# Two waits for GpSimd's first residual sums, and four VectorE normalisations moved behind the last lr-weighted writes

## The chip, the cores and the metric

The kernel runs on one core of a Trainium2 chip. The metric is device time in microseconds, the median of several executions. Beside it there is one profiled execution with its own time.

## The reference

`x` has 4 sequences of 1024 rows with 128 features, all in float32. Cut to what matters here:

```python
h  = layernorm(x)                                  # no gain, no offset
# delta block on h
z  = layernorm(h) * dn_g + dn_b
q, k, v = split(z @ gates_w + gates_b, 3);  lr = z @ lr_w + lr_b
k  = k / norm(k)
A  = tril(k @ k.T, -1) + eye;   u = solve_triangular(A, v, lower=True)
y  = (q @ k.T) @ (lr * u)                          # all 1024 rows of a sequence
h2 = h + y @ out_w + out_b
h3 = h2 + relu((layernorm(h2) * mn_g + mn_b) @ w1 + b1) @ w2 + b2
x1 = x + h3
# expert block on x1, 8 experts
n  = layernorm(x1);  e = argmax(n @ gate_w.T)
out = x1 + (n + n @ expert_w[e])   # as the reference writes it: x1 + ffn(n)
```

## The kernel before, in words

The 1024 rows are cut into T = 8 tiles of 128 rows; a tile holds NS = 4 sequences side by side (`n` = 0 to 3; LOW is 0 and 1, HIGH is 2 and 3). TG is 4, half of T. Each engine has a program of its own, written out by hand in order; semaphores are the only links between them, and an instruction that waits holds everything behind it on its engine.

There are three stages. First, keys, Gram matrices and the triangular inverses are made. Then comes a recurrence over the tiles: per tile and sequence, TensorE reads the state with the keys (`ks`), VectorE makes the residual values `rv` (L885), TensorE multiplies with the tile's inverse (`w_`, L1288, counted by `w_mm`), the product and its copy scaled with the learning rate `lr` go to the tile `ww`, and TensorE adds key times `ww` onto the state and onto the sum `m` (`s_`, L1298). For the last tile, t = T - 1, only the part scaled with `lr` is needed: ScalarE writes it for LOW (L626), VectorE for HIGH (L939, counted by `lrw_last`). The sums go through ScalarE's copy L631 (`mm`), a product with `wqT`, a copy to `mw` (L634 on ScalarE for LOW, L942 on VectorE for HIGH), a product with `wo`, and an addition (L947), to `gn`, which holds all that the last stage needs of the recurrence.

The last stage goes tile by tile. `delta(t)` on TensorE multiplies with `gn`; VectorE adds the residual `h_all` (`h2_`, L954), takes statistics (`hstats` L960, `haggr` L966), ScalarE takes the root (`hroot`, L638), VectorE makes the scale (`hscale`, L971) and the bias `nb2` (`hbias`, L975, counted by `hnb_done`, one per sequence), ScalarE normalises (`tn_`, L649, in `k_all`), TensorE turns the result (`tT_`), ScalarE copies it (L655), and two matrices follow (`hid_`, L1369, and `out_`, L1104). VectorE adds them to `x_all` (`x1_`, L981). The eight experts' products (L1390) and VectorE's predicated copies (L1022), which pick one of them, fill most of the rest. Tile 0 is worked in halves, LOW and HIGH; the others whole.

GpSimd (POOL) prepares `x_all` for `x1_`: `xb2_(t)` (L347) adds the constant `b2s`, `xb_(t)` (L353) adds `h_all` once `h2_` of that tile or half is written (`h2_ready`), and `x1_` waits for it through `xb_ready`. Before the last stage the residual `h_all` = `(x - mean) * scale` has to be made again: GpSimd does it for LOW (L340), VectorE for HIGH (`h_(t)`, L890, two instructions of 128x128 per tile, counted by `h_dve`). `xb2_(t)` and `h2_(t)` wait for both. VectorE's `h_` calls stand in its loop over the recurrence's tiles TG to T - 1, two of them, that is four instructions, per tile.

In the loop below, `rv_all(t)` is four times L885 and `yb`, `zb`, `t12` are parts of the inverses of the next tile.

Of the kernel before, what the change touches and what calls it, by code (L numbers as in the profile page):

```python
# [17 lines left out]
def delta_block_kernel(  # L18
# [19 lines left out]
    NS, L, C = x.shape  # L38
    E, F, _ = expert_w.shape
    T = L // P  # L40
# [3 lines left out]
    TG = T // NG  # L44
# [18 lines left out]
    with ExitStack() as ctx:  # L63
# [3 lines left out]
        def sem(name):  # L67
            return ctx.enter_context(nc.semaphore(name))
# [3 lines left out]
        def tiles(bank):  # L72
            return ps[:, bank, :].rearrange("p (n c) -> p n c", n=NS)

        def rows(t):
# [111 lines left out]
        hst_done, hmv_done, hsd_done, hrr_done, hnb_done = (sem("hst_done"), sem("hmv_done"), sem("hsd_done"),  # L187
                                                            sem("hrr_done"), sem("hnb_done"))
# [44 lines left out]
        def span(of):  # L233
            return slice(of[0], of[-1] + 1)

        def upto(t, of):
            return NS * t + of[-1] + 1
# [61 lines left out]
        @block.gpsimd  # L299
        def _(pool):  # L300
            nc.gpsimd.memset(ident[:], 0.0).then_inc(zeroed, 1)
            nc.gpsimd.memset(cent[:], 1.0 / C).then_inc(zeroed, 1)
            nc.gpsimd.memset(onec[:], 1.0)
            nc.gpsimd.memset(epsc[:], EPS).then_inc(consts_ready, 1)
            pool.wait_ge(zeroed, 1)
            nc.gpsimd.affine_select(out=ident[:], in_=ident[:], compare_op=ALU.not_equal, fill=1.0, base=0,
                                    pattern=[[-1, P]], channel_multiplier=1).then_inc(ident_ready, 1)
            pool.wait_ge(ident_ready, 1)
            pool.wait_ge(zeroed, 2)

            nc.gpsimd.tensor_tensor(cent[:], ident[:], cent[:], ALU.subtract).then_inc(cent_ready, 1)
            for g in range(NG):
                nc.gpsimd.memset(xi[g][:], 0.0).then_inc(xi_ready, 1)
            nc.gpsimd.memset(da_all[0:Q, :, :, Q:2 * Q].rearrange("p t n c -> p (t n) c"), 0.0).then_inc(da_clear, 1)
            for t in range(5, T):
                last = nc.gpsimd.memset(tt_all[:, t], 0.0)
            last.then_inc(tt_clear, 1)

            for t in range(1, T):
                pool.wait_ge(rr_done, PART[t] + 1)  # L320
                for n in XH_POOL[t]:
                    nc.gpsimd.tensor_scalar(xh[:, t, n], x_all[:, t, n], mv[:, 0, t, n, 0:1], rr[:, t, 1, n:n + 1],  # L322
                                            ALU.subtract, ALU.mult).then_inc(xh_pool, 1)


            pool.wait_ge(g_loaded, 16 * 2)
            pool.wait_ge(v_loaded, 16 * 5)
            nc.gpsimd.tensor_scalar(bmean[:], dnb.broadcast_to([P, P]), 1.0 / C, None, ALU.mult).then_inc(scaled_w, 1)
            for of in (slice(0, C), slice(2 * C, 3 * C + 1)):
                nc.gpsimd.tensor_scalar(gall[:, of], wall[:, of], dng, None, ALU.mult).then_inc(scaled_w, 1)  # L330


            pool.wait_ge(tt_dve, NG)
            pool.wait_ge(w_loaded, 16 * 8)

            nc.gpsimd.tensor_scalar(bob[:], bob[:], 1.0 / C, None, ALU.mult).then_inc(bo_ready, 1)  # L336
            pool.wait_ge(xT_mm, T)
            for t in range(T):
                for n in LOW:
                    last = nc.gpsimd.tensor_scalar(h_all[:, t, n], x_all[:, t, n], mv[:, 0, t, n, 0:1], rr[:, t, 0, n:n + 1],  # L340
                                                   ALU.subtract, ALU.mult)
                last.then_inc(h_pool, 1)

            def xb2_(t):
                pool.wait_ge(h_pool, t + 1)
                pool.wait_ge(h_dve, t + 1)
                nc.gpsimd.tensor_tensor(x_all[:, t], x_all[:, t], b2s[:, :].unsqueeze(1).broadcast_to([P, NS, C]),  # L347
                                        ALU.add).then_inc(xb2_ready, 1)

            def xb_(t, of=ALL):  # L350
                pool.wait_ge(h2_ready, upto(t, of))
                pool.wait_ge(xb2_ready, t + 1)
                nc.gpsimd.tensor_tensor(x_all[:, t, span(of)], x_all[:, t, span(of)], h_all[:, t, span(of)],  # L353
                                        ALU.add).then_inc(xb_ready, len(of))

            def add_(t):
                pool.wait_ge(scaled, t + 1)
                n = span(LOW if t == T - 1 else ALL)
                nc.gpsimd.tensor_tensor(x_all[:, t, n], x_all[:, t, n], sel[t % 2][:, n], ALU.add).then_inc(added, 1)  # L359

            for t in range(TG):
                xb2_(t)
            xb_(0, LOW)
            xb_(0, HIGH)
            xb_(1)
            for t in range(T):
                if TG <= t + 2 < T:
                    xb2_(t + 2)
                if t + 2 < T:
                    xb_(t + 2)  # L370
                if t > 0:
                    add_(t - 1)
            add_(T - 1)
# [345 lines left out]
        def _(dve):  # L719
# [145 lines left out]
            def yb(t):  # L865
                dve.wait_ge(yb_mm, t + 1)
                nc.vector.tensor_copy(yT[t % 2][2 * Q:3 * Q].rearrange("p n c -> p (n c)"),
                                      ps[2 * Q:3 * Q, 7, 0:NS * Q]).then_inc(yb_ready[1], 1)

            def zb(t):  # L870
                dve.wait_ge(zb_mm, t + 1)
                nc.vector.tensor_scalar(tt_all[2 * Q:3 * Q, t, :, 3 * Q:4 * Q],
                                        ps[2 * Q:3 * Q, 7, NS * Q:2 * NS * Q].rearrange("p (n c) -> p n c", n=NS), -1.0, None,
                                        ALU.mult).then_inc(zb_ready[1], 1)

            def t12(t):
                dve.wait_ge(t12_mm, t + 1)
                nc.vector.tensor_scalar(tt_all[0:2 * Q, t, :, 2 * Q:4 * Q],
                                        ps[0:2 * Q, 7, 2 * NS * Q:4 * NS * Q].rearrange("p (n c) -> p n c", n=NS), -1.0, None,
                                        ALU.mult).then_inc(t12_ready[1], 1)  # L880
# [7 lines left out]
            def h_(t):  # L888
                for n in HIGH:
                    last = nc.vector.tensor_scalar(h_all[:, t, n], x_all[:, t, n], mv[:, 0, t, n, 0:1], rr[:, t, 0, n:n + 1],  # L890
                                                   ALU.subtract, ALU.mult)
                last.then_inc(h_dve, 1)

            def rv_all(t):
                for n in range(NS):
                    rv_(t, n)
# [28 lines left out]
            for t in range(TG, T):  # L925
                if t > TG:
                    rv_all(t)
                if t + 1 < T:
                    yb(t + 1)
                    zb(t + 1)  # L930
                h_(2 * (t - TG))
                h_(2 * (t - TG) + 1)
                if t + 1 < T:
                    t12(t + 1)

            t = T - 1
            for n in HIGH:
                dve.wait_ge(w_mm, t * NS + n + 1)
                nc.vector.tensor_scalar(ww[t % 2][:, n, C:2 * C], ps[:, n, C:2 * C], v_all[:, t, n, C:VW], None,  # L939
                                        ALU.mult).then_inc(lrw_last, 1)  # L940
            dve.wait_ge(mw_mm, 2)
            nc.vector.tensor_copy(mw[:, 2:4], tiles(1)[:, 2:4]).then_inc(mw_ready[1], 1)  # L942

# [143 lines left out]
            t = T - 1  # L1087
# [369 lines left out]
```

## Time and profile before

| What | Value |
|---|---|
| median of 3 executions | 202.74 us (202.15 to 202.99) |
| the profiled execution's own time | 201.71 us |
| its span in the trace | 199.8 us |
| TensorE matmul busy | 179.8 us, 90% |
| VectorE busy | 166.3 us, 83% |
| ScalarE busy | 114.4 us, 57% |
| GpSimd busy | 63.7 us, 32% |

The span runs from the first to the last instruction of the trace, so the profiled execution has 1.91 us around it. TensorE is busy nearly everywhere, but not in every stretch: the recurrence and its passage into the last stage, from about 84 to 110 us, are chains over several engines. All times of the sections below count from the span's start.

### The profile page before, as it was taken

What the parts mean: (1) busy time and instruction counts of PE and PEld (TensorE: products, weight loads), DVE (VectorE), ACT (ScalarE), POOL (GpSimd) and SP (SyncE); (2) the same over time, 40 slices, a digit from 0 to 9 for tenths busy, and PEclk for the clock granted to TensorE, in tenths of its full rate; (3) what the DMA queues carried; (4) which work ended last, traced back from release to release, by engine and by line L of the source; (5) the groups of instructions that cost most, each with busy time, mean ns of one, the idle gap of its engine ahead of it and who ended that gap; (6) DMA issues with size and microseconds to landing.
All of it is one profiled execution on the core that took longest, in us unless ns stands there. A gap on an engine that the chain in (4) does not pass through costs nothing.

```text
span 199.8 us, 4189 instructions
## 1 busy us (share of the span) xinstructions
PE 179.8 (90%) x1299; PEld 130.7 (65%) x1299; DVE 166.3 (83%) x750; ACT 114.4 (57%) x318; POOL 63.7 (32%) x79
## 2 busy tenths in 40 slices
PE   0498799999999899999998999999999999999980
PEld 0355676887988677877864776766667675657540
DVE  7898899999899945494686688898989899878885
ACT  2567786588795785457327763645456363752420
POOL 8256980000000069980022220070605233202030
PEclk9999999999999999999999999999999999999997
DMA  4982011103000030000000000010101001011011
GB/s 115 302 211 29 10 16 20 21 5 59 3 2 3 0 61 1 3 3 3 0 2 0 3 0 0 0 54 3 53 0 36 18 5 53 0 53 53 0 54 53
DMA packets 20265, 6.53 MB, mean 33 GB/s; under 512 B 9995, under 2 KB 20244, under 8 KB 20244
## 3 DMA queue, kind: packets, MB, share of 16 engines
q1 hardware_dynamic: 19668, 6.21, 13.1%
q8 instruction: 10, 0.16, 0.4%
q10 hardware_dynamic: 576, 0.07, 0.2%
q14 instruction: 11, 0.09, 0.1%
HBM read 3.15 MB, written 2.10 MB: 26 GB/s over the span
## 4 chain that ended last, share of the span: by engine, by line
PE 62%; DVE 17%; ACT 5%; issue 3%; DVEq 0%; ACTq 0%
PE ps L1390 25%; PE ps L1104 10%; PE ps L1298 5%; PE ps L1099 5%; PE ps L1369 4%; DVE kT_all L1022 3%; DVE xi L836 3%; DVE prod L829 3%; PE ps L1133 2%; PE ps L1288 2%; DVE rv L885 2%; PE ps L1226 2%; PE ps L1282 2%; PE ps L1213 2%; PE ps L1116 1%
## 5 line engine op out<-in xcount | busy, mean ns | idle before, releaser
L1390 PE MATMUL ps<-ewC,kT_all 128*128 128x256 f32 (+2 forms) x192 | 62.0, 455 | 0.7 <-DVE kT_all L1022 0.7
L1022 DVE COPY_PREDICATED kT_all<-mask,ps 128x256 f32<-128x256 int32 x112 | 49.1, 439 | 2.6 <-DVE mask L1008 0.3
L1390 PEld LDWEIGHTS ps<-ewC,kT_all 128*128 128x128 f32 x192 | 33.9, 190 | 16.6 <-issue 6.0
L359 POOL TENSOR_TENSOR x_all<-x_all,kT_all 128x512 f32<-128x512 f32 (+1 forms) x8 | 9.6, 1204 | 54.6 <-ACT kT_all L679 54.6
L836 DVE TENSOR_TENSOR xi<-xi,prod 128x60 f32<-128x60 f32 (+13 forms) x116 | 19.6, 207 | 0.3
L829 DVE TENSOR_TENSOR prod<-lts,xi 128x60 f32<-128x60 f32 (+13 forms) x116 | 19.3, 204 | 0.3
L353 POOL TENSOR_TENSOR x_all<-x_all,h_all 128x512 f32<-128x512 f32 (+1 forms) x9 | 10.3, 1150 | 24.6 <-DVE h_all L954 19.9
L1298 PE MATMUL ps<-ww,k_all 128*128 128x256 f32 (+1 forms) x72 | 17.1, 365 | 0.4 <-DVE ww L939 0.4
L322 POOL TENSOR_SCALAR h_all<-x_all,mv,rr 128x128 f32<-128x128 f32 x18 | 14.6, 822 | 7.5 <-DVE rr L751 7.5
L649 ACT ACTIVATE k_all<-h_all,nb,rr 128x128 f32<-128x128 f32 x32 | 13.4, 483 | 1.9 <-DVE nb L975 1.5
L336 POOL TENSOR_SCALAR bob<-bob 128x128 f32<-128x128 f32 x1 | 0.5, 528 | 42.5 <-DVE da_all L859 42.5
L340 POOL TENSOR_SCALAR h_all<-x_all,mv,rr 128x128 f32<-128x128 f32 x16 | 12.5, 795 | 0.0
L1099 PE MATMUL ps<-ident,h_all 128*128 128x128 f32 x32 | 5.8, 312 | 7.3 <-ACT h_all L390 7.2
L1298 PEld LDWEIGHTS ps<-ww,k_all 128*128 128x128 f32 x72 | 11.1, 189 | 2.0 <-DVE ww L939 0.5
L1099 PEld LDWEIGHTS ps<-ident,h_all 128*128 128x128 f32 x32 | 4.4, 160 | 12.1 <-issue 12.0
L638 ACT ACTIVATE sd<-mv,epsc 128x4 f32<-128x4 f32 (+1 forms) x9 | 2.6, 294 | 15.0 <-DVE mv L966 15.0
L655 ACT ACTIVATE k_all<-ps,cols 128x512 f32<-128x512 f32 (+1 forms) x9 | 6.6, 730 | 8.1 <-PE ps L1099 8.1
L1104 PE MATMUL ps<-kT_all 128*128 128x128 f32 x64 | 9.5, 292 | 1.9 <-ACT kT_all L399 1.8
L679 ACT ACTIVATE kT_all<-kT_all,rr 128x128 f32<-128x128 f32 x30 | 9.5, 388 | 2.3 <-DVE kT_all L1022 2.3
L559 ACT ACTIVATE ww<-ww,v_all 128x128 f32<-128x128 f32 x28 | 10.7, 407 | 0.1
L666 ACT COPY kT_all<-ps 128x512 f32<-128x512 f32 (+1 forms) x9 | 4.8, 535 | 10.0 <-PE ps L1099 10.0
L1104 PEld LDWEIGHTS ps<-kT_all 128*128 128x128 f32 x64 | 8.0, 196 | 3.7 <-ACT kT_all L399 3.4
(156 smaller groups left out, 389.9 us busy)
## 6 DMA issues: line engine op xcount, KB each, us to landing
x_all<-in_L_attn_x_dram SPq DMA_DIRECT2D x7, 256.0 KB, 5.4
out_dram<-x_all SPq DMA_DIRECT2D x7, 256.0 KB, 2.3
ew<-in_L_ffn_expert_w_dram SPq DMA_DIRECT2D x1, 512.0 KB
gd<-gg_all SPq DMA_DIRECT2D x26, 16.0 KB, 1.8
tt_all<-dT_all SPq DMA_DIRECT2D x8, 48.0 KB, 2.1
x_all<-in_L_attn_x_dram SPq DMA_DIRECT2D x2, 128.0 KB, 2.8
out_dram<-x_all SPq DMA_DIRECT2D x2, 128.0 KB, 1.8
da_all<-d_all SPq DMA_DIRECT2D x4, 48.0 KB, 2.1
```

What stands on the lines that cost most here:

```text
L322: nc.gpsimd.tensor_scalar(xh[:, t, n], x_all[:, t, n], mv[:, 0, t, n, 0:1], rr[:, t, 1, n:n + 1], ALU.subtract, ALU.mult).then_inc(xh_pool, 1)
L340: last = nc.gpsimd.tensor_scalar(h_all[:, t, n], x_all[:, t, n], mv[:, 0, t, n, 0:1], rr[:, t, 0, n:n + 1], ALU.subtract, ALU.mult)
L353: nc.gpsimd.tensor_tensor(x_all[:, t, span(of)], x_all[:, t, span(of)], h_all[:, t, span(of)], ALU.add).then_inc(xb_ready, len(of))
L559: nc.scalar.mul(ww[t % 2][:, n, C:2 * C], ww[t % 2][:, n, 0:C], v_all[:, t, n, C:VW]).then_inc(lrw_ready, 1)
L649: nc.scalar.activation(tn[t % 2][:, n], h_all[:, t, n], ACT.Identity, bias=nb2[:, t, n:n + 1], scale=rr2[:, 0, t, n:n + 1]).then_inc(tn_re ...
L829: nc.vector.tensor_tensor(mul[half], lts[:, j, lo:hi].unsqueeze(2).broadcast_to([P, hi - lo, w]), xi[g][:, j, 0:w].unsqueeze(1).broadcast_ ...
L836: nc.vector.tensor_tensor(xi[g][:, lo:hi, 0:w], xi[g][:, lo:hi, 0:w], mul[half], ALU.subtract).then_inc(elim, 1)
L1022: nc.vector.copy_predicated(sel[t % 2][:, n], mask[t % 2][:, n, E - 1 - e].unsqueeze(2).broadcast_to([P, 2, F]), expert(e)).then_inc(picke ...
L1099: last = nc.tensor.transpose(tiles(bank)[:, n], src(n), ident[:])
L1104: last = nc.tensor.matmul(tiles(bank)[:, n], lhsT(n), rhs(n), start=True, stop=True)
L1298: last = nc.tensor.matmul(both(n)[:, of], k_all[:, t, n], ww[t % 2][:, n, of], start=t == 0 and n % 2 == 0 and of.start == 0, stop=True, s ...
L1390: last = nc.tensor.matmul(dst, x1T[t % 2][:, 2 * pair + n], ewC[:, of], start=True, stop=True)
```

## The change

Two additional waits stand in GpSimd's program: `xb_(0, LOW)` now also waits until the biases `nb2` of tile 0, LOW, are written, and `xb_(0, HIGH)` until those of all four sequences of tile 0 are. In VectorE's program the last four `h_` instructions, those of tiles T - 2 and T - 1, now follow the two writes of `ww` for the last tile, where they stood ahead of them. No instruction is added or removed.

```diff
@@ -360,7 +360,10 @@
 
             for t in range(TG):
                 xb2_(t)
+
+            pool.wait_ge(hnb_done, 2)
             xb_(0, LOW)
+            pool.wait_ge(hnb_done, NS)
             xb_(0, HIGH)
             xb_(1)
             for t in range(T):
@@ -928,9 +931,9 @@
                 if t + 1 < T:
                     yb(t + 1)
                     zb(t + 1)
-                h_(2 * (t - TG))
-                h_(2 * (t - TG) + 1)
                 if t + 1 < T:
+                    h_(2 * (t - TG))
+                    h_(2 * (t - TG) + 1)
                     t12(t + 1)
 
             t = T - 1
@@ -938,6 +941,8 @@
                 dve.wait_ge(w_mm, t * NS + n + 1)
                 nc.vector.tensor_scalar(ww[t % 2][:, n, C:2 * C], ps[:, n, C:2 * C], v_all[:, t, n, C:VW], None,
                                         ALU.mult).then_inc(lrw_last, 1)
+            h_(T - 2)
+            h_(T - 1)
             dve.wait_ge(mw_mm, 2)
             nc.vector.tensor_copy(mw[:, 2:4], tiles(1)[:, 2:4]).then_inc(mw_ready[1], 1)
 
```

VectorE's order of instructions before the change, from the residual values `rv` of the last tile to the second addition into `gn` (in `gg_all`); in brackets are the semaphores that an instruction waits for:

```order
L885 SCALAR_TENSOR_TENSOR rv<-v_all,nk,ps 128x128 [waits ks_mm] x4
L890 TENSOR_SCALAR h_all<-x_all,mv,rr 128x128 x4
L939 TENSOR_SCALAR ww<-ps,v_all 128x128 [waits w_mm] x2
L942 COPY gg_all<-ps 128x256 [waits mw_mm]
L947 TENSOR_TENSOR gg_all<-ps,bob 128x256 [waits gn_mm,bo_ready]
L947 TENSOR_TENSOR gg_all<-ps,bob 128x256 [waits gn_mm]
```

The same place in the changed kernel, whose lines have later numbers (L888 is L885 of before, L893 is L890, L942 is L939, L947 is L942, L952 is L947):

```order
L888 SCALAR_TENSOR_TENSOR rv<-v_all,nk,ps 128x128 [waits ks_mm] x4
L942 TENSOR_SCALAR ww<-ps,v_all 128x128 [waits w_mm] x2
L893 TENSOR_SCALAR h_all<-x_all,mv,rr 128x128 x4
L947 COPY gg_all<-ps 128x256 [waits mw_mm]
L952 TENSOR_TENSOR gg_all<-ps,bob 128x256 [waits gn_mm,bo_ready]
L952 TENSOR_TENSOR gg_all<-ps,bob 128x256 [waits gn_mm]
```

The four `h_all` instructions and the two of `ww` have changed places, and nothing else has moved on VectorE.

GpSimd's order before the change, from its last normalisations to the first addition of an expert's output (`sel`, in `kT_all`); the two rows of L353 with 128x256 are `xb_(0, LOW)` and `xb_(0, HIGH)`, folded into one:

```order
L340 TENSOR_SCALAR h_all<-x_all,mv,rr 128x128 x15
L347 TENSOR_TENSOR x_all<-x_all,b2s 128x512 [waits h_dve,h_pool] x4
L353 TENSOR_TENSOR x_all<-x_all,h_all 128x256 [waits xb2_ready,h2_ready] x2
L353 TENSOR_TENSOR x_all<-x_all,h_all 128x512 [waits xb2_ready,h2_ready] x3
L359 TENSOR_TENSOR x_all<-x_all,kT_all 128x512 [waits scaled]
```

And in the changed kernel:

```order
L340 TENSOR_SCALAR h_all<-x_all,mv,rr 128x128 x15
L347 TENSOR_TENSOR x_all<-x_all,b2s 128x512 [waits h_dve,h_pool] x4
L353 TENSOR_TENSOR x_all<-x_all,h_all 128x256 [waits h2_ready,xb2_ready,hnb_done] x2
L353 TENSOR_TENSOR x_all<-x_all,h_all 128x512 [waits xb2_ready,h2_ready] x3
L359 TENSOR_TENSOR x_all<-x_all,kT_all 128x512 [waits scaled]
```

Nothing moves within GpSimd's program; the two first sums have one more semaphore to wait for.

## Rows read from the trace of the kernel before

**Rows 1.** The page's head.

```profile
span 199.8 us, 4189 instructions
```

**Rows 2.** The chain that ended last, in order of time: start us, us, what.

```profile
97.28 0.27 DVE ww L939
...
105.31 1.24 DVE nb L975
...
109.83 0.44 PE ps L1099 x2
```

**Rows 3.** TensorE's timeline, 95 to 106 us: start, us, engine, line, what, [idle before].

```profile
95.61 1.20 PE L1288 MATMUL ps<-rv,tt_all 128*128 128x128 f32 x8
96.64 0.61 PE L1298 MATMUL ps<-ww,k_all 128*128 128x128 f32 x4
97.60 0.75 PE L1298 MATMUL ps<-ww,k_all 128*128 128x128 f32 x4 [0.35 <-DVE ww L939]
98.18 1.34 PE L1104 MATMUL ps<-wqT,gg_all 128*128 128x128 f32 x8
...
103.57 1.02 PE L1167 MATMUL ps<-ident,cent 128*128 128x512 f32 x2
```

**Rows 4.** VectorE's timeline, 96 to 110 us.

```profile
96.18 1.11 DVE L890 TENSOR_SCALAR h_all<-x_all,mv,rr 128x128 f32<-128x128 f32 x4
97.20 0.60 DVE L939 TENSOR_SCALAR ww<-ps,v_all 128x128 f32<-128x128 f32 x2
99.56 0.42 DVE L942 COPY gg_all<-ps 128x256 f32<-128x256 f32 x1 [1.75 <-PE ps L1104]
...
103.36 0.47 DVE L975 SCALAR_TENSOR_TENSOR nb<-mv,rr 128x2 f32<-128x2 f32 x1
...
104.43 0.69 DVE L954 TENSOR_TENSOR h_all<-ps,h_all 128x512 f32<-128x512 f32 x1
105.04 0.15 DVE L971 RECIPROCAL rr<-sd 128x2 f32<-128x2 f32 x1
105.31 1.23 DVE L975 SCALAR_TENSOR_TENSOR nb<-mv,rr 128x2 f32<-128x2 f32 x1
...
109.34 0.42 DVE L981 TENSOR_TENSOR x_all<-ps,x_all 128x256 f32<-128x256 f32 x1 [1.61 <-issue]
...
109.96 0.16 DVE L975 SCALAR_TENSOR_TENSOR nb<-mv,rr 128x4 f32<-128x4 f32 x1
```

**Rows 5.** GpSimd's timeline, 101 to 107 us.

```profile
101.92 0.72 POOL L353 TENSOR_TENSOR x_all<-x_all,h_all 128x256 f32<-128x256 f32 x1 [11.67 <-DVE h_all L954]
103.08 0.73 POOL L353 TENSOR_TENSOR x_all<-x_all,h_all 128x256 f32<-128x256 f32 x1 [0.44 <-DVE h_all L954]
105.26 1.27 POOL L353 TENSOR_TENSOR x_all<-x_all,h_all 128x512 f32<-128x512 f32 x1 [1.45 <-DVE h_all L954]
```

**Rows 6.** ScalarE's timeline, 98 to 107 us.

```profile
98.38 0.37 ACT L631 COPY gg_all<-ps 128x256 f32<-128x256 f32 x1 [0.73 <-PE ps L1298]
...
103.86 0.88 ACT L649 ACTIVATE k_all<-h_all,nb,rr 128x128 f32<-128x128 f32 x2 [0.88 <-DVE nb L975]
104.64 0.28 ACT L638 ACTIVATE sd<-mv,epsc 128x2 f32<-128x2 f32 x1
104.83 0.35 ACT L467 COPY ewC<-ps 128x256 f32<-128x256 f32 x1
...
105.34 0.57 ACT L655 ACTIVATE k_all<-ps,cols 128x256 f32<-128x256 f32 x1
106.58 0.88 ACT L649 ACTIVATE k_all<-h_all,nb,rr 128x128 f32<-128x128 f32 x2 [0.67 <-DVE nb L975]
```

**Rows 7.** Line L975 by itself: durations of its nine instructions.

```profile
L975 DVE SCALAR_TENSOR_TENSOR nb<-mv,rr x9: 150/153/1232, 103.4 to 170.6; 128x4 f32<-128x4 f32 x7, 128x2 f32<-128x2 f32 x2
```

**Rows 8.** VectorE's timeline at 85 us, a group of four L890.

```profile
85.44 3.39 DVE L890 TENSOR_SCALAR h_all<-x_all,mv,rr 128x128 f32<-128x128 f32 x4
```

**Rows 9.** Busy time by stretch: start:end length, PE, PEld, DVE, ACT, POOL, granted clock, DMA.

```profile
124.00:180.00 56.00, 55.50 (x249) 37.25 (x250) 49.84 (x197) 30.71 (x81) 16.38 (x13) 1.00 0.09 24
```

## The prediction on record

> **What bounds the kernel now.** I read the windows first. From 124 to 180 us TensorE's matmuls are busy 55.50 of 56.00 us at a granted clock of 1.00 [rows 9]: there the kernel runs at TensorE's pace, and whatever makes its first matmuls of that stage start earlier moves the whole stage earlier. The chain that ended last says the same: from 109.83 us on it stays on TensorE nearly to the end, while before that it goes over several engines. Two of its pieces are VectorE's: `ww` (L939) at 97.28, and a bias `nb2` (L975) that takes 1.24 us [rows 2]. The change is made at these two places. So I read the timelines of the engines between 95 and 110 us, and look in each for what a late instruction waited for.
>
> The first place. VectorE runs the four `h_` instructions from 96.18 to 97.29 (the row's 1.11 us) and then the two L939 [rows 4]. TensorE has ended the LOW half of the last `s_` (96.64 + 0.61 = 97.25) and starts the HIGH half at 97.60; the row gives the gap as 0.35 us and names L939 as what ended it [rows 3].
>
> The second place. L975 works on 2 or 4 numbers per partition. Its nine durations have a median of 153 ns, and the longest is 1232 ns [rows 7]. The two long ones are those of tile 0: LOW starts at 103.36 and takes 0.47, so ends at 103.83; HIGH starts at 105.31 and takes 1.23, so ends at 106.54 [rows 4]. GpSimd's sums L353 run from 103.08 to 103.81 and from 105.26 to 106.53 [rows 5]. Both L975 end within 0.02 us of the end of a sum that had started earlier. That is no work of their own but a wait for GpSimd's instruction, while the tile's L954 (one input from PSUM) and L971 (one input) show nothing like it. L975 and L353 both read two tensors in SBUF.
>
> [...]
>
> **The change part by part: A, the four `h_`.** They move behind L939. The third and fourth `w_` products end at about 96.51 and 96.81: the row of eight passes ends at 95.61 + 1.20 = 96.81, and each product is a quarter of that, about 0.3 us, earlier than the next [rows 3]. So L939 can run from about 96.55 to 97.19 (0.60 for both [rows 4], 0.04 from matmul to VectorE). That is before TensorE is through with the LOW half at 97.25. The gap of 0.35 us closes, and no more: VectorE is ready 0.65 us earlier, but TensorE isn't. By the pitch of the HIGH group (the next starts 0.58 after it, 98.18 - 97.60) LOW would let HIGH in at 97.22, a gain of 0.38; I take 0.35. Behind it, the HIGH copy on ScalarE (98.38 [rows 6]), the product with `wqT`, and L942 at 99.56 each follow on what came before, so all of them move by 0.35. The moved four then stand from about 97.2 to 98.3, while L942 is next due at 99.56 - 0.35 = 99.21: 0.9 us of cover. If that cover were gone, each further us would be paid. GpSimd has no instruction in the 11.67 us before 101.92 [rows 5], so nothing excludes the four there. Who waits for them: `h_dve` 7 and 8, needed by `xb2_` and `h2_` of tiles 6 and 7, tens of us later. Bounds of A: 0, if something else than L939 sets the HIGH half, and 0.65.
>
> **B, the two waits.** In the times of before, without A. `hbias` LOW takes 0.15 (the median of L975) in place of 0.47 and ends at 103.51: 0.32 earlier. VectorE works on without idling, so L954 of tile 1 starts at 104.11 and ends at 104.80. On ScalarE the first `tn_` (L649) moves from 103.86 to 103.54, the root L638 from 104.64 to 104.32; L971 follows at 104.72 and `hbias` HIGH at 104.99. It now meets no sum if `xb_(0, LOW)` is over: that one is released at 103.51, starts 0.14 later (as 105.26 does against the end of L954, 104.43 + 0.69 = 105.12), takes 0.72 and ends at 104.37. Margin 0.6 us. So `hbias` HIGH ends at 105.14 in place of 106.54: 1.40 us earlier.
>
> Not all of that is worth something, since ScalarE stands between. Before its next `tn_` (HIGH, 106.58) it has the copy L467, which waits for `expert_one(0)` on TensorE (103.57 + 1.02 = 104.59 [rows 3]), another copy, and L655 at 105.34 for 0.57. L467 was at 104.83 and can't go before about 104.63, so these three move by 0.20 only: L655 then ends at 105.14 + 0.57 = 105.71, and `tn_` HIGH starts at about 105.61 (ScalarE starts the next instruction some 0.1 before the one before ends, as 104.83 after 104.64 + 0.28 [rows 6]). That is 106.58 - 105.61 = 0.97 us. Everything up to `x1_` at 109.34 follows that instruction: the turn, its copy, the matrices. **B is worth 0.97 us**; its bounds are 0.5, if another link of that passage takes hold, and 1.40.
>
> What waits behind GpSimd's two waits: `xb_(0, HIGH)` goes from 105.28 to 106.01 and `xb_(1)`, directly behind it, to about 107.3. `x1_(0, LOW)` needs the first of the three (104.37) at 109.34 - 0.97 = 108.37. `hbias(1)`, the next L975, was at 109.96 [rows 4] and will be at 108.99; the last sum ends 1.7 us earlier. No DMA and no instruction is added. [...] No row here shows a wait's own cost.
>
> **The sum.** 0.35 + 0.97 = 1.32 us. The profiled execution took 201.71, its span 199.8 [rows 1] and 1.91 around it, which don't change: 200.39. The median of before is 202.74, 0.5% over the profiled one; in proportion, 202.74 x 200.39 / 201.71 = **201.4 us**. What comes behind TensorE's stage follows on it and moves along.
>
> **The rivals.**
> 1. Something behind `tn_` HIGH absorbs part of B: only 0.4 to 1.0 us come, 201.8 to 202.3. For it: the passage from 106.6 to 109.3 goes over three engines, ScalarE works in order, and its copies and roots stand between. Against it: each of them waits for an instruction that moves too. Chance 0.22.
> 2. The exclusion isn't the cause of the long L975, or is only moved to another instruction of the same chain: then A alone is left, 202.74 - 0.35 = 202.4. Against it: the two ends that agree to 0.02 us. Chance 0.05.
> 3. More than I count: the whole 1.40 of B and up to 0.65 of A, 2.05 together, 200.7. For it: ScalarE's three instructions might be pulled earlier. Against it: L467 and the HIGH half wait for TensorE. Chance 0.06.
> 4. Slower. The moved `h_` are late for L942. The same four took 3.39 us at 85.44 [rows 8], while GpSimd worked, in place of 1.11. They start at about 97.2; from 2.0 us of duration on they delay L942, and from 2.0 + 1.3 = 3.3 us on they eat up the whole gain. At 5 us each further us shows: 202.74 + 1.7 = 204.4. Against it: GpSimd is idle there. Chance 0.03.
>
> **How the numbers follow.** The forecast's own case (a gain of 1.0 to 1.7 us) has 0.64. A measurement of this kernel can tell about 0.5%, 1.0 us, from no change. Faster by more than that are the forecast's case and rival 3, 0.70. Within it are rivals 1 and 2, 0.27. Slower is rival 4, 0.03. The range reaches from nearly rival 3's end, 200.9, into rival 1, to 202.2; what is left out (rivals 2 and 4 and the ends of 1 and 3) is under 0.2.
>
> **What the profile of the changed kernel would show.** A: no idle time on TensorE ahead of the HIGH half of L1298; L942's successor starting some 0.35 earlier. B: no L975 over 0.2 us; the first sum of 128x256 on GpSimd beginning just behind the first L975, the second just behind the second; the second `tn_` about 1.3 us earlier than 106.58; TensorE's stage from 124 to 180 in the same pace and clock. I would be wrong if an L975 is still long (the exclusion is met elsewhere), if ScalarE idles ahead of the second `tn_` for a new reason, or if TensorE's stage lengthens by what was gained.

## The result, and the profile after

The changed kernel takes 200.98 us (median of 8 executions, 200.60 to 201.68) against 202.50 for the kernel before (8 executions, 201.68 to 203.09). The ratio is 0.9929, with a 95% interval of 0.9904 to 0.9953: a gain of 1.44 us by the ratio, where 1.32 was forecast (201.4 us, from a median of 202.74 for the kernel before). A second comparison later (the last experiment) gave 0.9949 (0.9927 to 0.9972).

The profiled execution took 201.12 us, its span is 199.0 where before it was 199.8 [rows 1]. That is only 0.8 us less, since this execution came to the changed part later. The first `rv` of the last tile stands at 95.77 in place of 95.14, though no instruction ahead of it was changed. So I measure distances in the trace, from that instruction on. The distances are from start to start: from the first `rv` of tile 7 to `h2_(0, LOW)`, from there to `x1_(0, LOW)`, and from there to the last transfer of the output that is issued. That issue, before and after:

```profile
197.54 0.37 SPq L296 DMA_DIRECT2D out_dram<-x_all  x1
```

```profile
196.81 0.37 SPq L296 DMA_DIRECT2D out_dram<-x_all  x1
```

| Kernel | rv to h2_ | h2_ to x1_ | x1_ to last issue | sum | first rv at |
|---|---|---|---|---|---|
| before | 6.22 | 7.98 | 88.20 | 102.40 | 95.14 |
| changed | 5.91 | 6.91 | 88.22 | 101.04 | 95.77 |

The sum falls by 1.36 us, and all of it ahead of `x1_(0, LOW)`. The ratio's interval allows 0.95 to 1.94 us, so that it comes out near the trace's value is partly luck; the second comparison gives 1.03. The page counts 4191 instructions where it was 4189 [rows 1]: the two waits count as instructions (4189 again with A alone, 4190 with one wait), and only they are added. VectorE's timeline of the changed kernel (start, us, engine, line, what, [idle before]) at the rows that answer to [rows 4]; lines are 3 to 5 higher than before:

```profile
95.77 1.12 DVE L888 SCALAR_TENSOR_TENSOR rv<-v_all,nk,ps 128x128 f32<-128x128 f32 x4
97.21 0.61 DVE L942 TENSOR_SCALAR ww<-ps,v_all 128x128 f32<-128x128 f32 x2 [0.32 <-PE ps L1293]
97.74 1.11 DVE L893 TENSOR_SCALAR h_all<-x_all,mv,rr 128x128 f32<-128x128 f32 x4
99.60 0.42 DVE L947 COPY gg_all<-ps 128x256 f32<-128x256 f32 x1 [0.75 <-PE ps L1109]
...
101.68 0.42 DVE L959 TENSOR_TENSOR h_all<-ps,h_all 128x256 f32<-128x256 f32 x1 [0.43 <-PE ps L1109]
...
103.68 0.16 DVE L980 SCALAR_TENSOR_TENSOR nb<-mv,rr 128x2 f32<-128x2 f32 x1
...
105.33 0.16 DVE L980 SCALAR_TENSOR_TENSOR nb<-mv,rr 128x2 f32<-128x2 f32 x1
...
108.59 0.42 DVE L986 TENSOR_TENSOR x_all<-ps,x_all 128x256 f32<-128x256 f32 x1 [1.90 <-issue]
```

The two biases take 0.16 us each, where they took 0.47 and 1.23. The four `h_` follow the two `ww`, and 0.75 us of idle time is left behind them. TensorE's timeline, the answer to [rows 3]:

```profile
97.27 1.10 PE L1303 MATMUL ps<-ww,k_all 128*128 128x128 f32 x8
98.43 1.13 PE L1109 MATMUL ps<-wqT,gg_all 128*128 128x128 f32 x8
...
103.62 1.02 PE L1172 MATMUL ps<-ident,cent 128*128 128x512 f32 x2
```

Both halves of the last `s_` now run without a gap. The product with `wqT` starts 98.43 - 95.77 = 2.66 us after the first `rv`, where it was 98.18 - 95.14 = 3.04: 0.38 us won. GpSimd and ScalarE, which answer to [rows 5] and [rows 6]:

```profile
103.97 0.72 POOL L353 TENSOR_TENSOR x_all<-x_all,h_all 128x256 f32<-128x256 f32 x1 [13.10 <-DVE nb L980]
105.62 1.95 POOL L353 TENSOR_TENSOR x_all<-x_all,h_all 128x256 f32<-128x256 f32 x2 [0.93 <-DVE nb L980]
```

```profile
97.91 0.86 ACT L634 COPY gg_all<-ps 128x256 f32<-128x256 f32 x2 [0.60 <-PE ps L1303]
99.15 0.37 ACT L637 COPY gg_all<-ps 128x256 f32<-128x256 f32 x1 [0.38 <-PE ps L1109]
...
103.88 0.88 ACT L652 ACTIVATE k_all<-h_all,nb,rr 128x128 f32<-128x128 f32 x2 [0.57 <-DVE nb L980]
104.66 0.28 ACT L641 ACTIVATE sd<-mv,epsc 128x2 f32<-128x2 f32 x1
104.85 0.35 ACT L470 COPY ewC<-ps 128x256 f32<-128x256 f32 x1
105.10 0.36 ACT L471 COPY ewC<-ps 128x256 f32<-128x256 f32 x1
105.36 0.57 ACT L658 ACTIVATE k_all<-ps,cols 128x256 f32<-128x256 f32 x1
105.82 0.88 ACT L652 ACTIVATE k_all<-h_all,nb,rr 128x128 f32<-128x128 f32 x2
```

GpSimd's first sum starts behind the first bias, 0.13 us after its end (103.97 against 103.68 + 0.16), and the next two behind the second one. ScalarE now has no idle time ahead of the second `tn_` (L652 at 105.82): there it had waited 0.67 us for the bias [rows 6]. The stage behind keeps its pace and clock; the window is 1 us earlier than in [rows 9], and as long:

```profile
123.00:179.00 56.00, 55.41 (x249) 37.12 (x249) 50.07 (x198) 30.68 (x81) 16.36 (x13) 1.00 0.09 24
```

### The profile page after: what moved, and what is told of

Its sections match the earlier page's. It is cut to its first block, busy times and chain, and to the rows that moved or that the text cites. A ratio compares the mean times of both kernels' runs of the same rounds, so it can differ in the third digit from the quotient of the medians.

```text
span 199.0 us, 4191 instructions
## 1 busy us (share of the span) xinstructions
PE 180.2 (91%) x1299; PEld 131.4 (66%) x1299; DVE 165.0 (83%) x750; ACT 114.4 (57%) x318; POOL 63.7 (32%) x79
## 4 chain that ended last, share of the span: by engine, by line
PE 66%; DVE 14%; ACT 5%; issue 2%; DVEq 0%; ACTq 0%
PE ps L1395 26%; PE ps L1109 10%; PE ps L1303 5%; PE ps L1104 5%; PE ps L1374 4%; DVE kT_all L1027 3%; DVE xi L839 3%; PE ps L1293 3%; DVE prod L832 3%; PE ps L1287 2%; PE ps L1138 2%; PE ps L1231 2%; DVE rv L888 2%; PE ps L1218 2%; PE ps L1121 1%
## 5 line engine op out<-in xcount | busy, mean ns | idle before, releaser
L353 POOL TENSOR_TENSOR x_all<-x_all,h_all 128x512 f32<-128x512 f32 (+1 forms) x9 | 10.3, 1152 | 23.3 <-DVE nb L980 14.0
L652 ACT ACTIVATE k_all<-h_all,nb,rr 128x128 f32<-128x128 f32 x32 | 13.4, 484 | 1.0 <-DVE nb L980 0.6
L1109 PE MATMUL ps<-kT_all 128*128 128x128 f32 x64 | 10.2, 307 | 2.0 <-ACT kT_all L402 1.9
L1109 PEld LDWEIGHTS ps<-kT_all 128*128 128x128 f32 x64 | 8.6, 208 | 3.9 <-ACT kT_all L402 3.6
```

The source lines that it names most:

```text
L652: nc.scalar.activation(tn[t % 2][:, n], h_all[:, t, n], ACT.Identity, bias=nb2[:, t, n:n + 1], scale=rr2[:, 0, t, n:n + 1]).then_inc(tn_re ...
L1109: last = nc.tensor.matmul(tiles(bank)[:, n], lhsT(n), rhs(n), start=True, stop=True)
```

## The experiments

Theory: VectorE's bias is held until the end of GpSimd's sum (106.54 against 106.53 in [rows 4] and [rows 5]), and is so since both read two tensors in SBUF (B; the expectations call this exclusion), and four `h_` stood in the way of `ww` (A). Rivals: one part brings all; any small instruction is held; any busy GpSimd holds; the wait for the bias isn't what delays ScalarE. Each kernel was timed on the same chip as the kernel before, on three chips in all, and each ratio is against that.

**A alone.** The kernel before with the diff's VectorE part only:

```diff
-                h_(2 * (t - TG))
-                h_(2 * (t - TG) + 1)
                 if t + 1 < T:
+                    h_(2 * (t - TG))
+                    h_(2 * (t - TG) + 1)
                     t12(t + 1)
...
+            h_(T - 2)
+            h_(T - 1)
             dve.wait_ge(mw_mm, 2)
```

> Part A alone (the four h_ behind L939; GpSimd waits as before). Theory of the prediction: no idle time on TensorE ahead of the HIGH half of the last s_, and from the first rv of tile 7 to h2_(0, LOW) 0.3 us less than before (6.22 there, 5.91 in the changed kernel); both L975 of tile 0 stay long (about 0.5 and 1.2 us). Gain 0.3 us, ratio 0.998 to 0.999. Rival: A brings most of the gain, because something else behind it moves more; then the ratio would be near 0.993 and L975 short.

Ratio 0.9993 (0.9973 to 1.0014), not told from no change by time. In the trace, `rv` to `h2_` is 5.92 us, `h2_` to `x1_` 7.97, together 0.31 shorter than before. Both biases are as long as they were, and the second ends with a sum of GpSimd (105.24 + 1.23 = 106.47, and 105.19 + 1.26 = 106.45). VectorE:

```profile
103.29 0.46 DVE L977 SCALAR_TENSOR_TENSOR nb<-mv,rr 128x2 f32<-128x2 f32 x1
...
105.24 1.23 DVE L977 SCALAR_TENSOR_TENSOR nb<-mv,rr 128x2 f32<-128x2 f32 x1
```

GpSimd in the same kernel:

```profile
105.19 1.26 POOL L353 TENSOR_TENSOR x_all<-x_all,h_all 128x512 f32<-128x512 f32 x1 [1.45 <-DVE h_all L956]
```

So A is worth 0.31 us, and the rival that it brings most of the gain is out.

**B alone.** The kernel before with the two waits:

```diff
+            pool.wait_ge(hnb_done, 2)
             xb_(0, LOW)
+            pool.wait_ge(hnb_done, NS)
             xb_(0, HIGH)
```

> Part B alone (GpSimd's two waits; the h_ where they were). Theory: both L975 at 0.16 us; from h2_(0, LOW) to x1_(0, LOW) 7.98 - 0.97 = 7.0 us, since ScalarE's copy L467 is held by expert_one(0) on TensorE; ratio about 0.995. In the changed kernel the same distance is 6.91: if A had a part in that (its earlier HIGH half lets TensorE's filling work run earlier), B alone gives 7.0; if my estimate of L467 was merely wrong, it gives 6.9. Rival: the waits bring nothing by themselves, ratio 1.000.

Ratio 0.9964 (0.9941 to 0.9988). `rv` to `h2_` stays at 6.22; `h2_` to `x1_` is 7.03: B alone is worth 0.95 us, where 0.97 was forecast. A and B together are worth 1.38 at `x1_`, 0.12 more than the sum of the two. The trace shows why. First TensorE, then ScalarE:

```profile
104.65 1.02 PE L1169 MATMUL ps<-ident,cent 128*128 128x512 f32 x2
```

```profile
105.42 0.28 ACT L640 ACTIVATE sd<-mv,epsc 128x2 f32<-128x2 f32 x1
105.71 0.37 ACT L469 COPY ewC<-ps 128x256 f32<-128x256 f32 x1
```

`expert_one(0)` ends at 105.67 and ScalarE's copy of its bank starts at 105.71, 0.29 after the root's start, where unhindered it is 0.19 (104.85 - 104.66 in the changed kernel). With A, TensorE gets to `expert_one(0)` earlier against `h2_` (103.62 - 101.68 = 1.94, against 104.65 - 102.44 = 2.21 here), so the copy isn't held. The delay goes on to `hid_(0, LOW)`, which waits for the copy behind (L657) and starts 4.53 us after `h2_` here (106.97 - 102.44), where in the changed kernel it is 4.39 (106.07 - 101.68).

**The first wait alone.** The changed kernel without its second wait:

```diff
             xb_(0, LOW)
-            pool.wait_ge(hnb_done, NS)
             xb_(0, HIGH)
```

> The changed kernel without its second wait: xb_(0, HIGH) runs directly behind xb_(0, LOW), at about 104.7 to 105.4, and xb_(1) follows h2_(1). Theory of exclusion: the second L975, due at 105.33, meets either the end of xb_(0, HIGH) (0.1 to 0.2 us lost) or, if xb_(1) gets in ahead of it, all of xb_(1), and then ends at 106.7: 1.2 us lost, ratio against before 0.994 to 0.999. Rival, that only the first wait matters: the second L975 at 0.16 us.

Ratio 0.9951 (0.9932 to 0.9970); the distances are 5.92 and 6.90, those of the changed kernel. The rival was right here: the second bias takes 0.16. VectorE and, in narrow windows, GpSimd:

```profile
105.14 0.16 DVE L979 SCALAR_TENSOR_TENSOR nb<-mv,rr 128x2 f32<-128x2 f32 x1
```

```profile
104.47 0.73 POOL L353 TENSOR_TENSOR x_all<-x_all,h_all 128x256 f32<-128x256 f32 x1
...
105.16 1.28 POOL L353 TENSOR_TENSOR x_all<-x_all,h_all 128x512 f32<-128x512 f32 x1
```

But the bias fell into the seam of two sums, 0.06 us ahead of the first one's end and 0.02 ahead of the second one's start.

**Off the seam.** As the run before, with a useless memset on GpSimd that moves `xb_(0, HIGH)` (128x192, 0.26 us; it writes a tile that nobody reads any more):

```diff
             xb_(0, LOW)
+            nc.gpsimd.memset(lts[:, 0:6], 0.0)
             xb_(0, HIGH)
```

> The run with the first wait alone, and a memset of 128x192 on GpSimd (about 0.2 us) between xb_(0, LOW) and xb_(0, HIGH). There the second bias started at 105.14, 0.02 us ahead of xb_(1), in the seam between two sums. Now xb_(0, HIGH) should run from about 104.7 to 105.4 and the bias start inside it. If it was the seam that spared it: the bias is held for at least 0.2 us more, and for about 1.5 us (0.8 to 1.0 us of it lost at x1_) if xb_(1) gets in ahead of it. If the second wait is of no use for another reason: 0.16 us again.

VectorE, then GpSimd:

```profile
104.97 0.28 DVE L980 SCALAR_TENSOR_TENSOR nb<-mv,rr 128x2 f32<-128x2 f32 x1
```

```profile
104.50 0.73 POOL L353 TENSOR_TENSOR x_all<-x_all,h_all 128x256 f32<-128x256 f32 x1
...
105.19 1.27 POOL L353 TENSOR_TENSOR x_all<-x_all,h_all 128x512 f32<-128x512 f32 x1
```

The bias starts inside the sum and ends at 105.25, behind the sum's end at 105.23: it is held for 0.12 us, and the next sum doesn't get in ahead of it. My worst case, 1.5 us, didn't occur. `h2_` to `x1_` is 6.91, so the 0.12 costs nothing: ScalarE is busy until later. Ratio 0.9953 (0.9931 to 0.9974). The second wait is thus of no measurable use at these times: what made the bias of 1.23 us was `xb_(1)`, and the first wait already makes that sum start later than the bias. It does so by 0.02 us in the run before and by 0.22 in this one, which is little: what happens when `xb_(1)` comes first again, as in the kernel before, no run with the first wait alone shows.

**One input in place of two.** A alone, and for tile 0 the bias made by an instruction with one tensor and a pointer scalar:

```diff
+                if t > 0:
                     nc.vector.scalar_tensor_tensor(nb2[:, t, span(of)], mv[:, 1, t, span(of), 0], -1.0, rr2[:, 0, t, span(of)],
                                                    ALU.mult, ALU.mult).then_inc(hnb_done, len(of))
+                    return
+                for n in of:
+                    nc.vector.tensor_scalar(nb2[:, t, n:n + 1], mv[:, 1, t, n, 0:1], rr2[:, 0, t, n:n + 1], -1.0,
+                                            ALU.mult, ALU.mult).then_inc(hnb_done, 1)
```

> A alone, and tile 0's biases made by one tensor_scalar of one element per sequence (one tensor in SBUF and a pointer scalar) in place of L975 with two tensors; GpSimd's sums run when they ran before. [...]

Ratio 0.9947 (0.9926 to 0.9969). The durations of the four new instructions (ns, min/median/max), and GpSimd's sums, which run when they ran before:

```profile
L982 DVE TENSOR_SCALAR nb<-mv,rr x4: 204/210/214, 103.3 to 105.2; 128x1 f32<-128x1 f32 x4
```

```profile
103.08 0.72 POOL L353 TENSOR_TENSOR x_all<-x_all,h_all 128x256 f32<-128x256 f32 x1 [0.43 <-DVE h_all L956]
105.05 1.27 POOL L353 TENSOR_TENSOR x_all<-x_all,h_all 128x512 f32<-128x512 f32 x1 [1.24 <-DVE h_all L956]
```

The run asks whether a bias made from one tensor in SBUF still ends with a sum. None is held, though the first two start inside the sum of 103.08 and the last inside that of 105.05. `h2_` to `x1_` is 7.00: nearly all of B without a wait on GpSimd. Each takes 0.21, more than the 0.15 of the bias with two tensors where nothing holds it [rows 7], and two in a row take 0.33 where one L980 takes 0.16. So it isn't any small instruction that is held: with the same sums over them the biases with two tensors in SBUF took 0.46 and 1.23 us (A alone), and these take 0.21. (The two forms also differ in operation and in the number of elements, 1 and 2; these were not varied by themselves.)

**A useless sum over the bias, and a memset in its place.** In the changed kernel, behind `xb_(0, LOW)`, one of these:

```diff
             xb_(0, LOW)
+            nc.gpsimd.tensor_tensor(lts[:, 0:16].rearrange("p (n a) b -> p n (a b)", n=NS), x_all[:, T - 1],
+                                    b2s[:, :].unsqueeze(1).broadcast_to([P, NS, C]), ALU.add)
             pool.wait_ge(hnb_done, NS)
```

```diff
             xb_(0, LOW)
+            nc.gpsimd.memset(lts[:], 0.0)
             pool.wait_ge(hnb_done, NS)
```

> The changed kernel, and one GpSimd sum of 128x512 of no use (it reads two tiles in SBUF and writes a dead one) right behind xb_(0, LOW), so that GpSimd is summing from about 104.7 to 105.9, over the moment of the second bias of tile 0 (105.33). Theory of exclusion: the second bias lasts until that sum's end, some 0.6 us, tn_ HIGH comes 0.3 to 0.5 us later than in the changed kernel, and the gain shrinks to about 0.9 us, ratio 0.995. Rival: two instructions do not exclude each other and the bias stays at 0.16.

> As the run before, with a memset of 128x1024 on GpSimd in place of the sum: it writes and reads nothing, and at 0.5 us for 128x512 it covers about 104.7 to 105.6. If it is GpSimd's reads that exclude VectorE's second input: bias 0.16 us, ratio as the changed kernel, 0.993. If any busy GpSimd holds it: 0.3 us for the bias.

With the sum, VectorE and GpSimd:

```profile
105.47 0.62 DVE L981 SCALAR_TENSOR_TENSOR nb<-mv,rr 128x2 f32<-128x2 f32 x1
```

```profile
104.80 1.27 POOL L366 TENSOR_TENSOR lts<-x_all,b2s 128x512 f32<-128x512 f32 x1
```

With the memset:

```profile
104.45 0.16 DVE L981 SCALAR_TENSOR_TENSOR nb<-mv,rr 128x2 f32<-128x2 f32 x1
```

```profile
103.76 0.95 POOL L366 MEMSET lts<- 128x1024 f32 x1
```

The sum ends at 106.07 and the bias at 106.09, so it lasts until the sum's end, 0.62 us, as forecast. Under the memset, which runs until 104.71, the bias takes 0.16. (The 0.5 us for a memset of 128x512 is what L316 takes in the kernel before, 0.51; this one of 128x1024 takes 0.95.) So the cost comes back with a sum, which reads two tensors, and not with a memset, which only writes. A GpSimd instruction that reads one was not tried. The price is small: with the sum, `tn_` HIGH starts 4.29 us after `h2_` (106.12 - 101.83) in place of 4.14, so 0.15 later and not 0.3 to 0.5, and `h2_` to `x1_` is 7.07 in place of 6.91. That is 0.16 of the 0.46 by which the bias is longer, since in the changed kernel ScalarE comes to that `tn_` only 0.33 us after the bias has ended (105.82 against 105.33 + 0.16). The ratios, 0.9941 (0.9919 to 0.9962) and 0.9926 (0.9897 to 0.9955), don't tell them apart.

**Sums over the moved h_.** The rival that ended slower, made to happen: in the changed kernel two useless sums, released by the first `ww`:

```diff
+            pool.wait_ge(lrw_last, 1)
+            for j in range(2):
+                nc.gpsimd.tensor_tensor(lts[:, 16 * j:16 * j + 16].rearrange("p (n a) b -> p n (a b)", n=NS),
+                                        x_all[:, T - 2 + j], b2s[:, :].unsqueeze(1).broadcast_to([P, NS, C]), ALU.add)
             pool.wait_ge(hnb_done, 2)
             xb_(0, LOW)
```

> The changed kernel, and two useless GpSimd sums of 128x512 released by the first of the two L942, so that they run from about 97.7 to 100.2, where the four moved h_ stand. This is the rival that ends slower, made to happen: the h_ are held, 2.5 to 3.5 us for the four in place of 1.11, the copy to mw behind them comes 0.7 to 1.7 us later than 99.60, h2_(0, LOW) 0.5 to 1.5 us later, ratio 0.995 to 1.000. If the h_ had cover enough or were not excluded: no difference to the changed kernel.

VectorE in this kernel:

```profile
98.66 2.99 DVE L896 TENSOR_SCALAR h_all<-x_all,mv,rr 128x128 f32<-128x128 f32 x4
101.57 0.41 DVE L950 COPY gg_all<-ps 128x256 f32<-128x256 f32 x1
```

In narrow windows, the first two of the four, and then the two sums:

```profile
98.66 1.25 DVE L896 TENSOR_SCALAR h_all<-x_all,mv,rr 128x128 f32<-128x128 f32 x1
...
99.83 1.30 DVE L896 TENSOR_SCALAR h_all<-x_all,mv,rr 128x128 f32<-128x128 f32 x1
```

```profile
98.56 1.27 POOL L366 TENSOR_TENSOR lts<-x_all,b2s 128x512 f32<-128x512 f32 x1 [6.77 <-DVE ww L945]
...
99.79 1.26 POOL L366 TENSOR_TENSOR lts<-x_all,b2s 128x512 f32<-128x512 f32 x1
```

Each of these two `h_` ends 0.08 us after a sum (99.91 against 99.83, 101.13 against 101.05). The four take 2.99 us in place of 1.11, the copy behind them starts 4.88 us after the first `rv` in place of 3.83, and `rv` to `h2_` is 6.60 in place of 5.91: 0.69 lost. Another 0.19 is lost behind `h2_`, where `expert_one(0)` (105.57 + 1.02 = 106.59) again holds ScalarE's copy, which starts at 106.63, 0.37 after the root. `rv` to `x1_` is 13.70 against 14.20 of before, ratio 0.9980 (0.9959 to 1.0001). The cover of 0.75 us is real and finite: 1.88 us more of `h_` delay the copy by 1.05 and `h2_` by 0.69.

**TensorE's filling work in halves.** A try to win more. The changed kernel with `expert_` and `expert_one` cut into halves of 256 columns, and in this order:

```diff
+            expert_(0, 0)
             pe.wait_ge(gn_ready[0], 1)
             delta(0, LOW)
             pe.wait_ge(gn_ready[1], 1)
             delta(0, HIGH, 3)
-            expert_(0)
+            expert_(0, 1)
             delta(1)
-            expert_one(0)
+            expert_one(0, 0)
+            expert_one(0, 1)
+            expert_(1, 0)
             tT_(0, LOW)
-            expert_(1)
+            expert_(1, 1)
+            expert_one(1, 0)
             hid_(0, LOW)
             tT_(0, HIGH, 6)
-            expert_one(1)
+            expert_one(1, 1)
```

> The changed kernel with TensorE's filling work (expert_ and expert_one, two of 128x512 each) cut in halves of 128x256: the first half stands in the gap of 0.58 us ahead of delta(0, LOW), one more ahead of tT_(0, LOW), and only one in place of two ahead of out_(0, LOW). If TensorE bounds the passage from 104.8 to 108.9 now, as its chain without gaps says, x1_(0, LOW) comes up to 0.43 us earlier after h2_(0, LOW) (6.5 in place of 6.91) and the ratio is 0.991. Rival: ScalarE's order bounds it, 6.8 to 6.9 and no difference.

`h2_` to `x1_` is 6.49, as forecast. But `rv` to `h2_` is 6.00, 0.09 more, and from `x1_` to the last issue it is 88.37 against 88.22. Of 0.42 us 0.18 are left, and the ratio is 0.9926 (0.9899 to 0.9954), the changed kernel's. Part of the loss shows right behind `x1_`: the second one, HIGH, comes 109.63 - 107.71 = 1.92 us later, where in the changed kernel it is 110.36 - 108.59 = 1.77, and TensorE waits 0.20 for ScalarE:

```profile
108.82 0.71 PE L1109 MATMUL ps<-w2s,k_all 128*128 128x128 f32 x4 [0.20 <-ACT k_all L664]
```

**The changed kernel again.**

> The changed kernel once more, on the same chip as the run beside it: both biases 0.16 us; 5.91 us from the first rv of tile 7 to h2_(0, LOW) and 6.91 from there to x1_(0, LOW), each within 0.03; ratio 0.993.

The distances are 5.92 and 6.90, both biases 0.16. The ratio is 0.9949 (0.9927 to 0.9972): 0.2% from the first one, with a trace that is the same to 0.03 us.

## Why the prediction was right

- **A, 0.35 forecast, 0.31 measured.** The gap closed, and the product with `wqT` came 0.38 earlier (the pitch's value). At `h2_` only 0.31 are left. ScalarE's copy to `mw` for LOW (L637) now waits 0.38 us for TensorE, whose four passes of that product take 0.68 us in place of 0.61. "All of them move by 0.35" was too simple: VectorE's copy for HIGH (L947) moved by 0.59, the LOW chain by 0.31, and the LOW one leads to `h2_`.
- **The cover of the moved four, 0.9 forecast, 0.75 measured**, since L947, behind them, moved by 0.59 and not by 0.35. The run with sums over them shows that more is paid once it is gone.
- **B, 0.97 forecast.** Alone it is 0.95; in the changed kernel it is 1.07. The bias itself ends 1.37 us earlier against `h2_` there (5.18 before, 105.33 + 0.16 - 101.68 = 3.81 after), where 1.40 was forecast. That less than this arrives was put down to L467 being held by `expert_one(0)`. The hold is real, but it is the smaller part, 0.12 us, and gone with A. The larger part, 0.30, is ScalarE's order: the root, the copies and L655 stand ahead of `tn_` HIGH, and they move only as far as the first bias lets them. The term that was mis-sized is "these three move by 0.20 only": alone L655 moves by 0.18 against `h2_` (106.24 - 102.44 = 3.80 against 105.34 - 101.36 = 3.98), in the changed kernel by 0.30 (105.36 - 101.68 = 3.68). I had costed B without A, and added the two.
- **TensorE sets the same limit**, which the prediction doesn't have. In the changed kernel its matmuls are busy 3.68 of the 3.69 us from 104.81 to 108.50, up to `x1_`, so by this trace a still earlier second bias would have brought no more. The 1.07 are the 0.30 by which `tT_(0, LOW)` moves and the 0.79 us of idle time ahead of `tT_(0, HIGH)`, to 0.02. The run with the filling work in halves bears it out: there `x1_` comes 0.42 earlier though the second `tn_` starts as before, 4.14 us after `h2_` (105.36 - 101.22, and 105.82 - 101.68).
- **The reading behind B** is right, but one step of it doesn't hold as it stands. L954 at 104.43 and L971 at 105.04 were to show that other instructions aren't held, yet no sum runs then: [rows 5] has none between 103.81 and 105.26. In the kernel before, these two do run under one (101.92 to 102.64 and 103.08 to 103.81), and take 0.42 and 0.17 as elsewhere:

```profile
102.52 0.42 DVE L954 TENSOR_TENSOR h_all<-ps,h_all 128x256 f32<-128x256 f32 x1
103.08 0.17 DVE L971 RECIPROCAL rr<-sd 128x2 f32<-128x2 f32 x1
```

- **The waits on GpSimd cost nothing**, as forecast: the last sum ends at 107.57, ahead of the next bias at 109.20, and the first starts 0.13 us after its release, where 0.14 was reckoned from the kernel before. A cost of the added semaphore is not seen. That both are needed was implied and is not so: the first alone gives the same distances.
- **The sum:** 1.32 forecast, 1.38 at `x1_`, 1.36 to the last issue, 1.44 by the first ratio and 1.03 by the second. That the sum is so near is in part luck: A came 0.04 short and B 0.10 over. The measured 200.98 us lies just inside the range (200.9 to 202.2); 0.24 of its distance from 201.4 is that the kernel before came out at 202.50 and not 202.74. The second `tn_` came 1.39 us earlier against `rv` (10.05 in place of 11.44), where about 1.3 was forecast.
- **Rival 1** (something absorbs part) did not happen, **rival 2** is refuted by B alone and by the runs with one input, the sum and the memset, **rival 3** was right in a small part (0.10 more). **Rival 4** needs a busy GpSimd; made to happen, it takes back 0.88 of 1.38 us and not the whole.

## What to carry to other kernels

The bias that took 1.23 us where it takes 0.15 otherwise, and ended 0.01 us after GpSimd's sum, was waiting and not working. Where a trace shows such a pair, look at what the other engine runs at that time. Three remedies are seen here: start the other one after it (bias 0.16 us), give it one SBUF tensor in place of two (0.21, shown for one element per partition; the `h_`, 128x128 with one tensor, are held all the same, to 1.25 and 1.30 us), or have the other engine only write (0.16 under the memset). Price such a repair at the next engines on the path: 1.38 us off the bias were 0.95 at `x1_` alone and 1.07 with the other repair. ScalarE's and TensorE's own instructions stood between, and without the other repair a filler on TensorE too. Two repairs of one passage are to be costed together.

## What the runs showed of the hardware

- VectorE's bias ends 0.02 us after the GpSimd sum that held it (106.09 against 106.07, 105.25 against 105.23). In the run off the seam GpSimd had another sum ready. That one didn't hold the waiting bias, which ended at 105.25, and wasn't late for it: it starts 0.69 us after the sum ahead of it (105.19 - 104.50), as in the run with the bias in the seam (105.16 - 104.47).
- The `h_` (128x128, one tensor in SBUF) are held by a sum, to 0.08 us after its end (99.91 against 99.83, 101.13 against 101.05), and the one-element instructions of the same kind (`TENSOR_SCALAR`, 0.21 us each) aren't. At which size that changes was not tried.
- The unchanged start of the kernel is what scatters. In the twelve profiled executions the first `rv` of tile 7 starts between 94.84 and 96.69 us, while its distance to VectorE's first big transpose is the same in before and after to 0.02 us (95.14 - 23.35 = 71.79 and 95.77 - 23.96 = 71.81). In all twelve that distance is 71.78 to 71.95 us, while the transpose starts between 22.99 and 24.82. So the scatter comes from the first 25 us, in which the inputs are loaded (in the kernel before, 115, 302, 211 and 29 GB/s in the first four slices of 5 us); what of it makes it was not tried. It is larger than the change. A alone, 0.31 us, can't be told by time (0.9973 to 1.0014), while the distances in the traces repeat to 0.03 us.
